# Graph attention on one core: sorted edges in groups of 128 instead of 256, and twice as many additions to the blocks' sums

## The chip, the cores and the metric

One core of a Trainium2 chip (trn2) runs the whole program. The metric is its time on the device in microseconds; the profile calls the engines PE (TensorE), DVE (VectorE), ACT (ScalarE), POOL (GpSimd) and SP (SyncE).

## What is computed

Two graph layers on 6250 nodes of 64 values with 200,000 directed edges; `dst` comes sorted, `src` doesn't. The change lies in the first, an attention over 400,000 entries (each edge both ways):

```python
idx = concatenate([edge_index, edge_index[:, ::-1]])      # 400,000 entries
src, dst = idx[:, 0], idx[:, 1]
gl, gr = (h @ Wl.T)[src], (h @ Wr.T)[dst]                 # 4 heads of 16
score = (att * leaky_relu(gl + gr, 0.2)).sum(-1)          # per head
ex = exp(score - segment_max(score, src)[src])
out = segment_sum(gr * ex / segment_sum(ex, src)[src], src)
x = x + gelu(concat([out, h]) @ W1.T + b1) @ W2.T + b2
```

The second layer sums `h[src] + edge_attr` by `dst` and ends with a normalisation over the nodes. The change leaves it alone.

## The kernel before

*Preparation and sort* (`prepare`, `Sort`, `decode`; up to about 1066 us). The entries are sorted on the chip by source node. Nodes stand in 49 blocks of 128. The entries of a block are filled up with padding to a whole number of groups of GROUP = 256, so that each group belongs to one block. `prepare` counts the entries of each block, adds them up to `ends`, and works out the block of each of the 1612 groups: a transpose of `ends` to a column, a comparison of 49 partitions with 1612 group numbers, four matmuls with ones, a limit, and a conversion to integers in `m.blk_i`, one partition (L383 to L389 on TensorE, L480 to L488 on VectorE).

*Attention* (`attention`, about 1066 to 5258 us). A step is 1024 sorted entries in 8 tiles of 128, and there are 403 steps in 13 chunks: twelve of 32 and one of 19. A score step q does this:

- GpSimd gathers the rows of `gr` by 8 indirect DMAs into one of 8 slots, tile by tile (L855).
- SyncE reads the block number of each of the 4 groups into a register and loads that block's `gl` table, 32 KB (L864, L866), up to 8 steps ahead.
- VectorE makes `hot_t`, one column of 128 for each entry (`hot_of`, L1010), four steps ahead (LAG); TensorE multiplies it with the table (`left`, L876) into bank q % 4.
- VectorE adds the gathered rows (L1062), ScalarE multiplies by the slope, VectorE takes the maximum (L1068), weighs with `att` (L1079) and sums over each head (the reduction of L139).

After the score steps of a chunk come a `scan` (the maximum of each node and the exponentials, L1085 to L1149) and then, during the score steps of the next chunk, the sum steps r of this one: weights to PSUM (`weight_of`, L1026), terms (`term_of`, L1035 and L1037), `hot_sum` (L1042), a matmul for each tile (`scatter`, L886) that sums a group over its two tiles, and one addition of 128x68 for each group into `m.acc` at the block of the group (`accumulate`, L1021). A score step takes one sum step along; a chunk with more sum steps than score steps has further ones in between (`sum_step`). The additions of step r are done at step r + 4. At a chunk's end those of its last four steps are done at once.

Each addition is made of these lines; the block number is read (L1017) right before it, and it waits for the addition before it:

```python
for i in groups:
    g = r * STEP_GROUPS + i
    blk = dve.value_load(m.blk_i[0:1, g:g + 1], min_val=0, max_val=BLOCKS - 1)
    sums = m.acc[:, bass.ds(blk, 1), :].rearrange("p b f -> p (b f)")
    at_least(dve, s_acc, g)
    dve.wait_ge(s_sum, r + 1)
    dve.tensor_tensor(sums, sums, sums_of(r % SUM_SLOTS, i), ALU.add).then_inc(s_acc, 1)
```

In `score_step` one addition follows each of four operations: the terms, L1068, `hot_of`, `hot_sum`. The sums of a step fill one of three banks (4 to 6); `scatter` of step r waits until the additions of step r - 3 are done. The scan uses banks 5 and 6 when all additions are through. The order on every engine is the order of the program text; semaphores stand for all dependences.

Of the kernel before, what the change touches and what calls it, by code (L numbers as in the profile page):

```python
# [24 lines left out]
P = 128  # L25
# [19 lines left out]
GROUP_TILES = 2  # L45
# [8 lines left out]
STEP_GROUPS = 4  # L54
STEP_TILES = STEP_GROUPS * GROUP_TILES
STEP = STEP_TILES * P
SIZES = [32] * 12 + [19]
# [84 lines left out]
def build(nc, t, out, stop=None):  # L142
    with ExitStack() as whole:
# [41 lines left out]
        m.blk_i = sb("blk_i", [1, GROUPS], I32)  # L185
        m.blk_f = sb("blk_f", [1, GROUPS], F32)
# [42 lines left out]
def prepare(m, ctx, sort):  # L229
# [16 lines left out]
    end_col = sb("end_col", [BLOCKS, 1], F32, ctx)  # L246
# [7 lines left out]
    iota_group = sb("iota_group", [BLOCKS, GROUPS], F32, ctx)  # L254
    past = sb("past", [BLOCKS, GROUPS], F32, ctx)
# [19 lines left out]
    s_end, s_end_ps = sem("s_end"), sem("s_end_ps")  # L275
    s_past, s_past_ps = sem("s_past"), sem("s_past_ps")
# [6 lines left out]
    with nc.Block() as block:  # L283
        @block.sync
        def _(sp):
            sp.wait_ge(s_init, 1)
            load_blocks(sp, m.x, t["x"], s_x)
            sp.wait_ge(s_init, 2)
            for dram, tile in ((t["src"], m.src), (t["dst"], m.dst)):
                sp.dma_start(tile[:, 0:FULL_COLS].rearrange("p (g t) -> p g t", t=EDGE_TILES),  # L290
                             dram[0:FULL_EDGES].rearrange("(g p t) -> p g t", p=P, t=EDGE_TILES)).then_inc(s_edges, 16)
                sp.dma_start(tile[0:TAIL_PARTS, FULL_COLS:EDGE_COLS],
                             dram[FULL_EDGES:E].rearrange("(p t) -> p t", t=EDGE_TILES)).then_inc(s_edges, 16)
            sp.wait_ge(s_init, 3)
# [3 lines left out]
            sp.wait_ge(s_grt, 32)  # L298

# [35 lines left out]
        def _(pool):  # L335
# [6 lines left out]
            pool.iota(iota_group[:, :], [[1, GROUPS]], base=0, channel_multiplier=0,  # L342
# [15 lines left out]
        def _(pe):  # L358
# [23 lines left out]
            pe.wait_ge(s_end, 1)  # L382
            pe.transpose(bank[6][0:BLOCKS, 0:P], ends[:, :], m.ident[:, :]).then_inc(s_end_ps, 1)  # L383
            pe.wait_ge(s_past, 1)
            part = GROUPS // 4
            for i in range(4):
                last = pe.matmul(bank[4 + i][:, 0:part], m.ones[0:BLOCKS, :], past[:, i * part:(i + 1) * part],
                                 start=True, stop=True)
            last.then_inc(s_past_ps, 1)  # L389
# [3 lines left out]
        def _(dve):  # L393
# [71 lines left out]
            dve.tensor_tensor_scan(ends[:, :], m.ones[:, 0:BLOCKS], counts[:, :], 0.0, ALU.mult,  # L465
                                   ALU.add).then_inc(s_end, 1)
# [17 lines left out]
            part = GROUPS // 4  # L484
            for i in range(4):
# [260 lines left out]
def attention(m, ctx):  # L746
# [13 lines left out]
    hot_t = [sb(f"hot_t{k}", [P, STEP], F32, ctx) for k in range(LAG)]  # L760
# [72 lines left out]
    def sums_of(slot, i):  # L833

        return bank[4 + slot][:, i * HEADS * ACCW:(i + 1) * HEADS * ACCW]
# [9 lines left out]
    with nc.Block() as block:  # L845
# [24 lines left out]
        def _(pe):  # L870
            def left(q):

                pe.wait_ge(s_hot, q + 1)
                pe.wait_ge(s_gl[q % U], loads(q, U) * STEP_GROUPS)
                for g in range(STEP_TILES):
                    last = pe.matmul(bank[q % LAG][:, g * D:(g + 1) * D], hot_t[q % LAG][:, g * P:(g + 1) * P],  # L876
                                     gl_s[q % U][:, g // GROUP_TILES, :], start=True, stop=True)
                last.then_inc(s_left, 1)
# [39 lines left out]
            for q in range(LAG):  # L918
                left(q)
            for c in range(CHUNKS + 1):  # L920
                for q, sums in turn_steps(c):
                    if q is not None and q + LAG < STEPS:
                        left(q + LAG)
# [11 lines left out]
        def _(act):  # L935
# [25 lines left out]
            for q in range(LAG + 2):  # L961
                load_place(q)
# [23 lines left out]
            for c in range(CHUNKS + 1):  # L986
                for q, sums in turn_steps(c):
                    if q is not None:
                        load_place(q + LAG + 2)
                        keep(q)  # L990
                        act.wait_ge(s_z, q + 1)
                        nc.scalar.mul(left_of(q % LAG), z[:, :, :], SLOPE).then_inc(s_low, 1)  # L992
# [7 lines left out]
        def _(dve):  # L1000
# [4 lines left out]
            def hot_of(q):  # L1005
# [4 lines left out]
                dve.tensor_tensor(hot_t[q % LAG][:, :], place_b[q % V][:, :], node_ps.to_broadcast([P, STEP]),  # L1010
                                  ALU.is_equal).then_inc(s_hot, 1)
# [32 lines left out]
            def sum_step(r, base):  # L1044

                weight_of(r, base)
                term_of(r)
                if r - LAG >= base:
                    accumulate(r - LAG, (0, 1))
                hot_sum_of(r)  # L1050
                if r - LAG >= base:
                    accumulate(r - LAG, (2, 3))

            def score_step(q, c, r, base):
# [3 lines left out]
                if r is not None:  # L1058
                    weight_of(r, base)
                dve.wait_ge(s_left, q + 1)  # L1060
# [99 lines left out]
            for q in range(LAG):  # L1160
                hot_of(q)

            for c in range(CHUNKS + 1):
# [469 lines left out]
```

## Time and profile before

| | us |
|---|---|
| median of 3 runs | 7368.41 (7367.21 to 7369.56) |
| profiled execution | 7364.49 |
| its span, first to last instruction | 7362.5 |
| VectorE busy | 4363.1 (59%) |
| GpSimd busy | 4625.4 (63%) |
| TensorE busy, matmuls | 4204.2 (57%) |
| attention, first table load to last addition | 1065.9 to 5257.8 |

Shares of busy time are means over stages of different kinds. Register and semaphore instructions of an engine's queue are not counted as busy; where they hold an engine up, it shows as idle time before the next instruction. A line of a group of instructions gives busy time and the mean of one; behind the bar stands the idle time of the engine in front of them and what ended it. TensorE's granted clock in the attention is 0.50, its lower level of 1.2 GHz.

### The profile page before, as it was taken

The page shows a single profiled execution, that of the slowest core. Times are in us where ns is not written, and L with a number is a line of the kernel's source. Part 1 is how long each engine was busy: PE and PEld are TensorE (multiplying, and loading weights), DVE is VectorE, ACT ScalarE, POOL GpSimd, SP SyncE. Part 2 cuts the span into 40 slices and gives each one's busy share as a digit, 9 for nine tenths or more (in the row PEclk, how much of TensorE's full clock was granted, in tenths as well). Part 3 has the DMA queues.
Part 4 walks back from the last instruction along what each step waited for, and adds up shares of the span by engine and source line. Part 5 has one row for each costly group of instructions (what it writes and reads, how often), then busy time and mean ns, then how long its engine had stood idle before and what let it go on. Part 6 is the DMA issues. An engine that isn't in the chain of part 4 may idle for free. (4 is left out here: it accounts for less than half of the span.)

```text
span 7362.5 us, 75948 instructions
## 1 busy us (share of the span) xinstructions
PE 4204.2 (57%) x18919; PEld 4018.0 (55%) x18919; DVE 4363.1 (59%) x7419; ACT 702.3 (10%) x1007; POOL 4625.4 (63%) x4809
## 2 busy tenths in 40 slices
PE   2011114567676777776677776768634445565666
PEld 1011114566676766666676766668533444555665
DVE  9999973667676676767667676768612222222332
ACT  6201100000000000000000000000100000000001
POOL 0000047777777777777777777775077777777774
PEclk9975555555555555555555555555655555555555
DMA  2000024444444444444444444443122222222221
GB/s 36 0 0 0 0 58 102 111 119 120 107 129 109 125 118 118 117 115 123 105 131 117 119 118 117 121 103 113 52 52 53 53 53 55 52 53 52 55 53 30
DMA packets 631935, 600.55 MB, mean 82 GB/s; under 512 B 382434, under 2 KB 385634, under 8 KB 631222
## 3 DMA queue, kind: packets, MB, share of 16 engines
q10 hardware_dynamic: 177888, 320.64, 13.7%
q0 software_dynamic: 153344, 157.33, 11.8%
q1 hardware_dynamic: 300246, 117.47, 6.4%
q8 instruction: 167, 2.74, 0.2%
q14 instruction: 290, 2.38, 0.1%
HBM read 480.76 MB, written 114.19 MB: 81 GB/s over the span
## 5 line engine op out<-in xcount | busy, mean ns | idle before, releaser
L855 POOL DMA_INDIRECT rows<-gr_table,row_of x3192 | 3075.4, 963 | 976.4 <-issue 970.8
L886 PE MATMUL bank<-terms,hot_sum 128*128 128x68 f32 x6448 | 1467.9, 423 | 774.2 <-DVE acc L1021 770.3
L886 PEld LDWEIGHTS bank<-terms,hot_sum 128*128 128x128 f32 x6448 | 1409.1, 331 | 822.6 <-DVE hot_sum L1042 817.1
L1371 POOL DMA_INDIRECT edge_rows<-h_table,src_sb x1568 | 1480.8, 944 | 531.4 <-issue 477.5
L876 PE MATMUL bank<-gl_step,hot_t 128*128 128x64 f32 x6448 | 1458.6, 421 | 280.5 <-DVE hot_t L1010 191.7
L876 PEld LDWEIGHTS bank<-gl_step,hot_t 128*128 128x128 f32 x6448 | 1421.5, 333 | 291.4 <-DVE hot_t L1010 278.3
L1392 PE MATMUL bank<-message,edge_hot 128*128 128x64 f32 x3136 | 714.6, 423 | 877.4 <-DVE message L1454 877.4
L1392 PEld LDWEIGHTS bank<-message,edge_hot 128*128 128x128 f32 x3136 | 683.5, 330 | 908.5 <-issue 908.5
L1062 DVE TENSOR_TENSOR fore<-bank,rows 128x512 f32<-128x512 f32 x403 | 277.7, 689 | 1037.0 <-DMA rows<-gr_table,row_of 1034.9
L1454 DVE TENSOR_TENSOR message<-bank,edge_rows 128x512 f32<-128x512 f32 x196 | 135.5, 692 | 1071.3 <-DMA edge_rows<-h_table,src_sb 1068.6
L696 POOL DMA_INDIRECT rows<-gr_table,row_of x32 | 50.1, 1567 | 958.5 <-DVE row_of L727 949.0
L992 ACT ACTIVATE bank<-fore 128x512 f32<-128x512 f32 x403 | 242.5, 602 | 3376.6 <-DVE fore L1062 3376.6
L1042 DVE TENSOR_TENSOR hot_sum<-bank,place 128x1024 f32<-128x1024 f32 x403 | 490.6, 1217 | 0.2 <-issue 0.2
L1010 DVE TENSOR_TENSOR hot_t<-place_b,bank 128x1024 f32<-128x1024 bf16 x403 | 489.1, 1214 | 1.5 <-DMA place_b<-place_rows 1.0
L1021 DVE TENSOR_TENSOR acc<-acc,bank 128x68 f32 x1612 | 354.2, 220 | 183.4 <-DVE acc L1021 133.8
L639 PE MATMUL bank<-ident,keys 128*128 128x128 f32 x448 | 95.9, 403 | 589.8 <-DVEq L624 500.4
L639 PEld LDWEIGHTS bank<-ident,keys 128*128 128x128 f32 x448 | 86.8, 216 | 599.8 <-DVEq L624 506.2
L1392 PE MATMUL bank<-message,edge_hot_more 128*128 128x64 f32 x1536 | 340.3, 423 | 50.4 <-DVE edge_hot_more L1423 50.4
L1392 PEld LDWEIGHTS bank<-message,edge_hot_more 128*128 128x128 f32 x1536 | 331.2, 332 | 59.4 <-DVE edge_hot_more L1423 59.4
L139 DVE TENSOR_REDUCE scores<-top 128x32 f32<-128x512 f32 x403 | 276.5, 686 | 59.5 <-DVE top L1079 1.0
L1417 ACT COPY bank<-edge 128x512 f32<-128x512 f32 x196 | 115.4, 589 | 1839.9 <-DVE message L1454 1823.2
L1068 DVE TENSOR_TENSOR fore<-fore,bank 128x512 f32<-128x512 f32 x403 | 274.5, 681 | 21.3 <-ACT bank L992 21.3
(267 smaller groups left out, 3211.9 us busy)
## 6 DMA issues: line engine op xcount, KB each, us to landing
place_b<-place_rows ACTq DMA_DIRECT2D x403, 256.0 KB
gr_rows<-rows ACTq DMA_DIRECT2D x403, 256.0 KB, 2.1
rows_again<-gr_rows ACTq DMA_DIRECT2D x403, 256.0 KB
rows<-gr_table,row_of POOLq DMA_INDIRECT x3224
gl_step<-gl_table SPq DMA_DIRECT2D x1612, 32.0 KB
edge<-in_edge_attr SPq DMA_DIRECT2D x97, 512.0 KB, 3.5
edge_rows<-h_table,src_sb POOLq DMA_INDIRECT x1568, 2.5
pen_s<-pen_rows ACTq DMA_DIRECT2D x52, 64.0 KB
```

Of the source, the lines that this page charges most:

```text
L139: return dve.tensor_reduce(out, in_, AX.X, op)
L855: pool.indirect_dma_start(rows[k][:, g, :], None, m.gr_table[:, :], bass.IndirectOffsetOnAxis(m.row_of[:, tile:tile + 1], 0)).then_inc(s_g ...
L876: last = pe.matmul(bank[q % LAG][:, g * D:(g + 1) * D], hot_t[q % LAG][:, g * P:(g + 1) * P], gl_s[q % U][:, g // GROUP_TILES, :], start=T ...
L886: last = pe.matmul(sums_of(r % SUM_SLOTS, g // GROUP_TILES), hot2[r % LAG][:, g, :], by_tile[:, g, :], start=g % GROUP_TILES == 0, stop=g ...
L992: nc.scalar.mul(left_of(q % LAG), z[:, :, :], SLOPE).then_inc(s_low, 1)
L1010: dve.tensor_tensor(hot_t[q % LAG][:, :], place_b[q % V][:, :], node_ps.to_broadcast([P, STEP]), ALU.is_equal).then_inc(s_hot, 1)
L1021: dve.tensor_tensor(sums, sums, sums_of(r % SUM_SLOTS, i), ALU.add).then_inc(s_acc, 1)
L1042: dve.tensor_tensor(hot2[r % LAG][:, :, :], places, at, ALU.is_equal).then_inc(s_summed, 1)
L1062: dve.tensor_tensor(z[:, :, :], left_of(q % LAG), rows[q % U][:, :, :], ALU.add).then_inc(s_z, 1)
L1068: dve.tensor_tensor(leaky[:, :, :], z[:, :, :], left_of(q % LAG), ALU.max).then_inc(s_leaky, 1)
L1371: pool.indirect_dma_start(rows[h % U][:, e, :], None, m.h2_table[:, :], bass.IndirectOffsetOnAxis(m.src[:, tile:tile + 1], 0)).then_inc(s_ ...
L1392: done = pe.matmul(out[:, 0:D], one_hot[:, e, :], messages_s[g % V][:, way, e, :], start=first and e == 0, stop=last and e == HALF - 1)
```

## The change

A group has 128 entries instead of 256 and a step 8 groups of one tile instead of 4 of two. A step stays 1024 entries. With smaller groups there is less padding: 397 steps instead of 403, the last chunk has 13 instead of 19, and 3176 groups stand for 1612.

- Each tile's matmul in `scatter` now stands alone, and each of the 8 groups has an addition of its own; SyncE loads 8 tables a step.
- The 8 sums of a step don't fit one bank; they take two, so there are two slots (banks 3 to 6) for three, and `scatter` of r waits for the additions of r - 2. The `left` products have three slots (LEFT) for four, with `hot_t` made three steps ahead.
- The additions of a score step stand in pairs at the four old places. The block numbers of a pair are read before the operation that the pair follows: for the first pair behind `weight_of`, for the others right behind the pair before. In `sum_step` there are two runs of four.
- The block of a group is found by comparing 25 group numbers on each of 128 partitions with the 49 ends, a reduction and a limit; a small DMA of SyncE brings the result to one partition. The transpose, the matmuls and the four limits on one partition go.

The core of the diff:

```diff
-GROUP_TILES = 2
+GROUP_TILES = 1
-STEP_GROUPS = 4
+STEP_GROUPS = 8
-SIZES = [32] * 12 + [19]
+SIZES = [32] * 12 + [13]
 LAG = 4
+LEFT = 3
-SUM_SLOTS = 3
+SUM_SLOTS = 2
+PART_GROUPS = -(-GROUPS // P)
...
-            dve.wait_ge(s_end_ps, 1)
-            c.link(dve.tensor_copy(end_col[:, :], bank[6][0:BLOCKS, 0:1]))
-            dve.tensor_scalar(past[:, :], iota_group[:, :], end_col[:, 0:1], None, ALU.is_ge).then_inc(s_past, 1)
-            dve.wait_ge(s_past_ps, 1)
-            part = GROUPS // 4
-            for i in range(4):
-                c.link(dve.tensor_scalar(m.blk_f[:, i * part:(i + 1) * part], bank[4 + i][0:1, 0:part],
-                                         float(BLOCKS - 1), None, ALU.min))
-            c.link(dve.tensor_copy(m.blk_i[:, :], m.blk_f[:, :]))
+            c.link(dve.tensor_tensor(past[:, :, :], iota_group[:, :].unsqueeze(2).to_broadcast([P, PART_GROUPS, BLOCKS]),
+                                     ends[:, :].unsqueeze(1).to_broadcast([P, PART_GROUPS, BLOCKS]), ALU.is_ge))
+            c.link(nc_reduce(dve, block_f[:, :], past[:, :, :]))
+            dve.tensor_scalar(block_of[:, :], block_f[:, :], float(BLOCKS - 1), None, ALU.min).then_inc(s_block, 1)
...
+            sp.wait_ge(s_block, 1)
+            sp.dma_start(m.blk_i[0:1, :].rearrange("o (p g) -> o p g", p=P), block_of[:, :]).then_inc(s_block_row, 16)
...
     def sums_of(slot, i):
-        return bank[4 + slot][:, i * HEADS * ACCW:(i + 1) * HEADS * ACCW]
+        half = STEP_GROUPS // 2
+        return bank[3 + 2 * slot + i // half][:, i % half * HEADS * ACCW:(i % half + 1) * HEADS * ACCW]
...
-            def accumulate(r, groups):
-                for i in groups:
-                    g = r * STEP_GROUPS + i
-                    blk = dve.value_load(m.blk_i[0:1, g:g + 1], min_val=0, max_val=BLOCKS - 1)
+            def blocks_of(r, groups):
+                return [dve.value_load(m.blk_i[0:1, r * STEP_GROUPS + i:r * STEP_GROUPS + i + 1], min_val=0, max_val=BLOCKS - 1)
+                        for i in groups]
+            def accumulate(r, groups, blocks):
+                dve.wait_ge(s_sum, r + 1)
+                for i, blk in zip(groups, blocks):
                     sums = m.acc[:, bass.ds(blk, 1), :].rearrange("p b f -> p (b f)")
-                    at_least(dve, s_acc, g)
-                    dve.wait_ge(s_sum, r + 1)
+                    at_least(dve, s_acc, r * STEP_GROUPS + i)
                     dve.tensor_tensor(sums, sums, sums_of(r % SUM_SLOTS, i), ALU.add).then_inc(s_acc, 1)
...
             def score_step(q, c, r, base):
                 if r is not None:
                     weight_of(r, base)
+                if add:
+                    blocks = blocks_of(r - LAG, (0, 1))
                 dve.wait_ge(s_left, q + 1)
                 dve.wait_ge(s_gath[q % U], loads(q, U) * STEP_TILES)
-                dve.tensor_tensor(z[:, :, :], left_of(q % LAG), rows[q % U][:, :, :], ALU.add).then_inc(s_z, 1)
+                dve.tensor_tensor(z[:, :, :], left_of(q % LEFT), rows[q % U][:, :, :], ALU.add).then_inc(s_z, 1)
                 if r is not None:
                     term_of(r)
                 if add:
-                    accumulate(r - LAG, (0,))
+                    accumulate(r - LAG, (0, 1), blocks)
+                    blocks = blocks_of(r - LAG, (2, 3))
                 dve.wait_ge(s_low, q + 1)
-                dve.tensor_tensor(leaky[:, :, :], z[:, :, :], left_of(q % LAG), ALU.max).then_inc(s_leaky, 1)
+                dve.tensor_tensor(leaky[:, :, :], z[:, :, :], left_of(q % LEFT), ALU.max).then_inc(s_leaky, 1)
                 if add:
-                    accumulate(r - LAG, (1,))
+                    accumulate(r - LAG, (2, 3), blocks)
+                    blocks = blocks_of(r - LAG, (4, 5))
-                hot_of(q + LAG)
+                hot_of(q + LEFT)
                 if add:
-                    accumulate(r - LAG, (2,))
+                    accumulate(r - LAG, (4, 5), blocks)
+                    blocks = blocks_of(r - LAG, (6, 7))
                 if r is not None:
                     hot_sum_of(r)
                 if add:
-                    accumulate(r - LAG, (3,))
+                    accumulate(r - LAG, (6, 7), blocks)
...
                     for r in range(START[c] - LAG, START[c]):
-                        accumulate(r, range(STEP_GROUPS))
+                        accumulate(r, range(STEP_GROUPS), blocks_of(r, range(STEP_GROUPS)))
```

## Rows read from the trace of the kernel before

**Rows 1.** Three stretches: us; busy PE, PEld, DVE, ACT, POOL; clock, DMA share, GB/s.

```profile
1377.70:4965.20 3587.50, 2532.07 (x11528) 2470.38 (x11528) 2431.51 (x4941) 264.74 (x407) 2725.71 (x2828) 0.50 0.45 118
4965.20:5175.20 210.00, 169.54 (x776) 165.72 (x776) 169.80 (x381) 15.33 (x24) 112.28 (x119) 0.50 0.36 104
5175.20:5257.80 82.60, 68.72 (x304) 66.05 (x304) 55.62 (x153) 0.91 (x1) 0.00 (x0) 0.50 0.17 49
```

**Rows 2.** Groups by line, 1100 to 5050: busy, mean ns | idle before, releasers.

```profile
L855 POOL DMA_INDIRECT rows<-gr_table,row_of x3114 | 3001.8, 964 | 949.1 <-issue 947.3 <-DVE fore L1062 1.8
```

**Rows 3.** Waits, 1100 to 5050: us in total, times, longest us.

```profile
DVE fore L1062 <- DMA rows<-gr_table,row_of: 1034.9, 292, 5.5
```

**Rows 4.** Line L1062, 4640 to 4664, then 1377 to 4966: durations; first, last start.

```profile
L1062 DVE TENSOR_TENSOR fore<-bank,rows x5: 680/681/687, 4640.9 to 4663.8; 128x512 f32<-128x512 f32 x5
...
L1062 DVE TENSOR_TENSOR fore<-bank,rows x353: 679/692/712, 1377.7 to 4965.2; 128x512 f32<-128x512 f32 x177
```

**Rows 5.** Timeline of VectorE after a scan: start us, us, instruction.

```profile
4676.58 0.68 DVE L1062 TENSOR_TENSOR fore<-bank,rows 128x512 f32<-128x512 f32 x1
4677.88 0.22 DVE L1021 TENSOR_TENSOR acc<-acc,bank 128x68 f32 x1
4678.01 0.68 DVE L1068 TENSOR_TENSOR fore<-fore,bank 128x512 f32<-128x512 f32 x1
...
4678.89 1.22 DVE L1010 TENSOR_TENSOR hot_t<-place_b,bank 128x1024 f32<-128x1024 bf16 x1
...
4681.43 0.68 DVE L1079 TENSOR_TENSOR top<-fore,bank 128x512 f32<-128x512 f32 x1
4682.25 0.69 DVE L139 TENSOR_REDUCE scores<-top 128x32 f32<-128x512 f32 x1
4682.95 0.68 DVE L1062 TENSOR_TENSOR fore<-bank,rows 128x512 f32<-128x512 f32 x1
```

**Rows 6.** Timeline of VectorE, first and last addition at a chunk's end.

```profile
4926.32 0.23 DVE L1021 TENSOR_TENSOR acc<-acc,bank 128x68 f32 x1 [0.15 <-issue]
...
4938.77 0.22 DVE L1021 TENSOR_TENSOR acc<-acc,bank 128x68 f32 x1 [0.60 <-DVE acc L1021]
```

**Rows 7.** Line L1088, the scan's first, 4640 to 5200.

```profile
L1088 DVE CAST edge_cols<-pen_s x2: 153/154/154, 4939.0 to 5150.7; 128x1 f32<-128x1 bf16 x2
```

**Rows 8.** Timeline of VectorE in the last sums.

```profile
5224.83 0.69 DVE L1035 TENSOR_TENSOR terms<-rows_again,bank 128x512 f32<-128x512 f32 x1
...
5227.81 0.22 DVE L1021 TENSOR_TENSOR acc<-acc,bank 128x68 f32 x1
5228.22 0.22 DVE L1021 TENSOR_TENSOR acc<-acc,bank 128x68 f32 x1 [0.19 <-DVE acc L1021]
...
5228.68 0.69 DVE L1035 TENSOR_TENSOR terms<-rows_again,bank 128x512 f32<-128x512 f32 x1
```

**Rows 9.** VectorE's queue, lines L1017, L1020 and L1021, whole span.

```profile
L1017 DVEq TENSOR_LOAD <-blk_i x1612: 296/303/992, 1402.8 to 5256.8; - x180
L1017 DVEq FUSED_REGOPS  x1612: 183/183/210, 1403.4 to 5257.2; - x180
L1017 DVEq SEQ_ASSERT  x1612: 23/23/41, 1403.7 to 5257.4; - x180
...
L1020 DVEq EVENT_SEMAPHORE  x1611: 21/21/21, 1404.6 to 5257.5; - x179
...
L1021 DVEq FUSED_REGOPS  x1612: 64/64/71, 1403.8 to 5257.5; - x180
```

**Rows 10.** TensorE's queue, line L1357, 5328 to 5331, two readings in a row.

```profile
L1357 PEldq TENSOR_LOAD <-step_of x2: 306/402/497, 5328.9 to 5329.7; - x2
```

**Rows 11.** Timeline of SyncE's queue, 1100 to 1115.

```profile
1100.34 14.76 SPq L866 DMA_DIRECT2D gl_step<-gl_table  x14
```

**Rows 12.** Timeline of the preparation, VectorE.

```profile
244.10 0.15 DVE L481 COPY end_col<-bank 49x1 f32<-49x1 f32 x1
...
254.60 0.27 DVE L552 TENSOR_TENSOR keys<-keys 128x64 f32<-128x64 f32 x1
```

More of the change, by code:

```diff
@@ L253, in prepare @@
     bias = sb("bias", [P, BLOCKS], F32, ctx)
-    iota_group = sb("iota_group", [BLOCKS, GROUPS], F32, ctx)
-    past = sb("past", [BLOCKS, GROUPS], F32, ctx)
+    iota_group = sb("iota_group", [P, PART_GROUPS], F32, ctx)
+    past = sb("past", [P, PART_GROUPS, BLOCKS], BF16, ctx)
+    block_f = sb("block_f", [P, PART_GROUPS], F32, ctx)
+    block_of = sb("block_of", [P, PART_GROUPS], I32, ctx)
     ordinal = sb("ordinal", [P, GROUP_TILES], F32, ctx)
@@ L381, in _ @@
             pe.matmul(bank[5][:, 0:BLOCKS], m.ones[:, :], below[:, :], start=True, stop=True).then_inc(s_cnt_ps, 1)
-            pe.wait_ge(s_end, 1)
-            pe.transpose(bank[6][0:BLOCKS, 0:P], ends[:, :], m.ident[:, :]).then_inc(s_end_ps, 1)
-            pe.wait_ge(s_past, 1)
-            part = GROUPS // 4
-            for i in range(4):
-                last = pe.matmul(bank[4 + i][:, 0:part], m.ones[0:BLOCKS, :], past[:, i * part:(i + 1) * part],
-                                 start=True, stop=True)
-            last.then_inc(s_past_ps, 1)
             sort.tensor(pe)
@@ L464, in _ @@
             c.link(dve.tensor_scalar(counts[:, :], counts[:, :], 1.0 / GROUP, None, ALU.mult))
-            dve.tensor_tensor_scan(ends[:, :], m.ones[:, 0:BLOCKS], counts[:, :], 0.0, ALU.mult,
-                                   ALU.add).then_inc(s_end, 1)
+            c.link(dve.tensor_tensor_scan(ends[:, :], m.ones[:, 0:BLOCKS], counts[:, :], 0.0, ALU.mult, ALU.add))
             dve.wait_ge(s_const, 6)
@@ L759, in attention @@
     place_b = [sb(f"place_b{k}", [P, STEP], BF16, ctx) for k in range(V)]
-    hot_t = [sb(f"hot_t{k}", [P, STEP], F32, ctx) for k in range(LAG)]
+    hot_t = [sb(f"hot_t{k}", [P, STEP], F32, ctx) for k in range(LEFT)]
     gl_s = [sb(f"gl_step{k}", [P, STEP_GROUPS, D], F32, ctx) for k in range(U)]
@@ L875, in left @@
                 for g in range(STEP_TILES):
-                    last = pe.matmul(bank[q % LAG][:, g * D:(g + 1) * D], hot_t[q % LAG][:, g * P:(g + 1) * P],
+                    last = pe.matmul(bank[q % LEFT][:, g * D:(g + 1) * D], hot_t[q % LEFT][:, g * P:(g + 1) * P],
                                      gl_s[q % U][:, g // GROUP_TILES, :], start=True, stop=True)
@@ L916, in scan @@
                 last.then_inc(s_back_ps, 1)
-            for q in range(LAG):
+            for q in range(LEFT):
                 left(q)
@@ L921, in _ @@
                 for q, sums in turn_steps(c):
-                    if q is not None and q + LAG < STEPS:
-                        left(q + LAG)
+                    if q is not None and q + LEFT < STEPS:
+                        left(q + LEFT)
                     for r in sums:
@@ L959, in keep @@
                               rows[q % U][:, :, :].rearrange("p g f -> p (g f)")).then_inc(s_store[q % U], 16)
-            for q in range(LAG + 2):
+            for q in range(LEFT + 2):
                 load_place(q)
@@ L1009, in hot_of @@
                 dve.wait_ge(s_place[q % V], loads(q, V))
[L1010 removed]
+                dve.tensor_tensor(hot_t[q % LEFT][:, :], place_b[q % V][:, :], node_ps.to_broadcast([P, STEP]),
                                   ALU.is_equal).then_inc(s_hot, 1)
[L1013 to L1017 removed]
+            def blocks_of(r, groups):
[4 more added lines that the diff above has]
+                for i, blk in zip(groups, blocks):
                     sums = m.acc[:, bass.ds(blk, 1), :].rearrange("p b f -> p (b f)")
[L1019 to L1020 removed]
+                    at_least(dve, s_acc, r * STEP_GROUPS + i)
                     dve.tensor_tensor(sums, sums, sums_of(r % SUM_SLOTS, i), ALU.add).then_inc(s_acc, 1)
@@ L1044, in sum_step @@
             def sum_step(r, base):
+                add = r - LAG >= base
                 weight_of(r, base)
+                if add:
+                    blocks = blocks_of(r - LAG, range(4))
                 term_of(r)
-                if r - LAG >= base:
-                    accumulate(r - LAG, (0, 1))
+                if add:
+                    accumulate(r - LAG, range(4), blocks)
+                    blocks = blocks_of(r - LAG, range(4, 8))
                 hot_sum_of(r)
-                if r - LAG >= base:
-                    accumulate(r - LAG, (2, 3))
+                if add:
+                    accumulate(r - LAG, range(4, 8), blocks)
             def score_step(q, c, r, base):
@@ L1059, in score_step @@
                     weight_of(r, base)
+                if add:
+                    blocks = blocks_of(r - LAG, (0, 1))
                 dve.wait_ge(s_left, q + 1)
                 dve.wait_ge(s_gath[q % U], loads(q, U) * STEP_TILES)
-                dve.tensor_tensor(z[:, :, :], left_of(q % LAG), rows[q % U][:, :, :], ALU.add).then_inc(s_z, 1)
+                dve.tensor_tensor(z[:, :, :], left_of(q % LEFT), rows[q % U][:, :, :], ALU.add).then_inc(s_z, 1)
                 if r is not None:
@@ L1159, in _ @@
             chain.link(dve.memset(inits[:, :, :], -BIG))
-            for q in range(LAG):
+            for q in range(LEFT):
                 hot_of(q)
```

16 lines of the change are left out of this document (6 added, 10 removed).

## The prediction

> **What bounds the kernel now.** I read the stages first [rows 1]. The first row is chunks 1 to 11 of the attention, 352 steps in 3587.5 us; the next is chunk 12 with its scan, the last the sums that are left. Then comes GpSimd's line for this stage [rows 2]: 3114 gathers, busy 3001.8 us, idle 949.1, nearly all of it issue (947.3) and only 1.8 us for a buffer. A gather therefore costs 1.27 us, a step of eight 10.15 us, and GpSimd is never held: it sets the pace of chunks 0 to 11. The list of waits says the same from VectorE's side [rows 3]: 1034.9 us of waiting for rows, about 86 us for each of the 12 chunks or so that the window holds. That is all the room the change has on VectorE before VectorE sets the pace.
>
> Where a chunk has its room is seen from the starts of the first operation of a score step (L1062). Just after a scan the gathers are ahead and VectorE runs unhindered: four steps without additions to acc take 22.9 us, 5.7 each [rows 4]; a step with four additions takes 6.37 (4676.58 to 4682.95) [rows 5]. Later it waits, and the chunk comes out at 3587.5 / 11 = 326.1 us [rows 1, 4].
>
> In chunk 12 and after it things differ: 185.5 us from its first score step (4965.2) [rows 4] to its scan (5150.7) [rows 7], where GpSimd is busy 112 of 210 us and VectorE 170 [rows 1]. VectorE's own work sets the time there, and afterwards no gather is left at all.
>
> **The change, part by part.** *Fewer steps.* 403 become 397: 48 gathers less, 48 x 1.27 = 61 us of GpSimd. All of them come off chunk 12 (19 steps become 13), which GpSimd does not bound. Its 32 sum steps stay. What can be gained there is VectorE's time alone.
>
> *Additions, 1612 to 3176.* Today one addition stands between two large operations and delays the next by 0.13 us (4677.88 to 4678.01), since its block number is read while the large operation ahead of it runs [rows 5]. In the change they come in pairs, and the second waits on s_acc until the first is done. The trace has that once nearly bare: 0.41 us from start to start (5227.81 to 5228.22) [rows 8]. From below, a dependent pair without an address (L1079 to L139) leaves 0.14 us after the end [rows 5], so 0.22 + 0.14 = 0.36. I take 0.39.
>
> *Where the block numbers are read.* This decides the forecast. A reading is three instructions on VectorE's queue: 0.303 + 0.183 + 0.023 = 0.509 us [rows 9]. The old order is: large operation, reading, addition. The new one is: additions, two readings, large operation. A large operation is handed over only when both readings in front of it are through, and they can't start early, because in front of them stands the address of the second addition, which waits for the first. So 0.22 us of addition is all the engine has to cover two readings. What an uncovered reading costs is seen at a chunk's end, where 16 additions stand with nothing between: 12.45 / 15 = 0.83 us each, 0.60 of it idle [rows 6]. Of the 0.83, 0.021 + 0.064 are the wait and the address [rows 9], so a reading is between 0.51 and 0.74; I take the middle, 0.62. Two in a row don't overlap on TensorE's queue, where the one such place has them 0.8 us apart [rows 10].
>
> From the second addition to the next large operation is thus 0.83 - 0.09 + 0.62 = 1.36 us, where it was 0.13. Each of the first three pairs adds 0.39 + 1.36 - 0.13 = 1.62; the fourth, with no readings behind it, 0.39. The first pair's readings stand behind the copy of the weights, beside the last reduction: from that reduction's start to the next L1062 took 0.70 us (4682.25 to 4682.95) [rows 5] and will take 0.1 + 1.24 + 0.1 = 1.44, so 0.74 more. A score step goes from 6.37 to 6.37 + 4.86 + 0.39 + 0.74 = 12.36 us. That is above the gathers' 10.15: VectorE becomes the bound and GpSimd waits.
>
> The Trainium skill, Perfetto Trace Analysis (Per-engine timelines), says that a VectorE instruction waits for semaphores in a queue of its own while the sequencer goes on, but that an instruction of the sequencer alone holds it until its semaphores are there. By the first half alone the readings would run ahead and the step would stay under the gathers' time (rival 1); the second half goes with the forecast, as L1021 has a register operation of its own ahead of each addition [rows 9].
>
> *A chunk.* Four steps without additions 22.9; 27 periods of 12.36, 333.7; from the last L1062 to the end of its reduction 12.36 - 1.44 + 0.69 = 11.6. At the chunk's end four steps are added at once: each 8 x 0.62 + 0.2 + 7 x 0.39 = 7.9, together 31.6 (13 today, 16 x 0.83). From scan start (4939.0) to the next chunk (4965.2) 26.2 as now [rows 4, 7]. Sum 426 for 326.1, times 11: +1099 us.
>
> *Chunk 12.* Two steps without additions 11.4, eleven with 136.0. A sum step takes 3.85 today (5224.83 to 5228.68) [rows 8]; less its additions (0.83, 0.41 and twice 0.13) 2.35 of other work. With eight readings, 4.96, and two runs of four additions, 6 x 0.39 = 2.34, it takes 9.65; 17 of them 164, two without additions 4.7; the end 31.6, less 1.4 for one head too many: 346 for 185.5, +161. *After it,* 13 sum steps: 4 x 2.35 + 9 x 9.65 + 31.6 = 128 for 82.6 [rows 1], +45.
>
> *Left slots three, sum banks in two slots.* The sums of step r now wait for the additions of r - 2 instead of r - 3, and behind them in TensorE's queue stands the next left product. TensorE is busy 2532 / 352 = 7.2 us a step [rows 1]: sums and left product are through some 7.3 us after those additions, and VectorE asks for them after the rest of that step (2.4) and a whole further one (12.36). Cost nothing; with a step of 7.9 (rival 1) still covered, by 3 us.
>
> *Table loads, eight a step.* SyncE, when nothing holds it, issues one every (14.76 - 0.33) / 13 = 1.11 us [rows 11], 8.9 a step: under 10.15 and 12.36, so hidden, except in chunk 0, where VectorE has no sums to do. There 32 x 8.9 = 284 us put the last scores some 10 us later than now: +10, between 0 and 20. The 51 MB more fit beside a DMA share of 0.45 [rows 1].
>
> *Blocks of the groups.* The stretch from 244.10 to 254.60 [rows 12] becomes a comparison and a reduction of 1225 elements (1.4 us each by L1010's 1.22 for 1024 [rows 5]) and a clamp of 0.2: 10.5 less 3.0, -7.5. The row's DMA has the whole sort as cover.
>
> Sum: 1099 + 161 + 45 + 10 - 7.5 = +1307 us, on the profiled execution's 7364.5 us; the median shown lies 3.9 above it: 8675 us.
>
> **The rivals.** *1. Readings hidden.* If the queue runs ahead, a step is 6.37 + 4 x 0.39 = 7.9, under 10.15, and eleven chunks stay at 326. Chunk 12: 11.4 + 11 x 7.9 + 4.7 + 17 x 4.7 + 31.6 = 215, +29; after it 9.4 + 9 x 4.7 + 31.6 = 83, nothing; with -7.5: 7390. For it: readings do run under large operations today [rows 5]. Against: there they stand behind one in the order.
>
> *2. Readings in a row cheaper.* [...] If each costs the 0.30 of the load alone [rows 9], a step is 12.36 - 8 x 0.32 = 9.8 and a chunk 22.9 + 264.6 + 56 = 343.5, +191; chunk 12 is 256 readings x 0.32 = 82 shorter, +79; after it 33 shorter, +12: 7368 + 275 = 7643. Against: the checks stand after every load [rows 9].
>
> *3. Faster.* If each added addition costs 0.13 and readings nothing anywhere, a score step is 6.9 and a sum step 2.35 + 8 x 0.13 = 3.4: chunk 12 is 11.4 + 75.9 + 4.7 + 57.8 + 13 = 163, -22; after it 9.4 + 30.6 + 13 = 53, -30; with -7.5: 7309. It decides while the additions of the 37 steps there cost under 1.6 us a step more than that; the idle 0.60 at the chunk's end [rows 6] speaks against it.
>
> **How the numbers follow.** Forecast 0.86, rival 1 0.05, rival 2 0.05, rival 3 0.02, within 0.2% (about what a measurement tells from no change) 0.02. Within the forecast every one of 3176 readings is bare: 0.51 for 0.62 takes 350 us off, 0.36 for 0.39 some 50; 0.74 would add 380, which I cut to 225, since the gaps between register operations are short. Range 8300 to 8900. Faster 0.03, same 0.03, slower 0.94.
>
> **What the profile would show.** Right: L1062's starts 12 us apart in mid-chunk and no wait for rows after a chunk's first steps; GpSimd idle with L1062 as releaser, some 100 us a chunk; three gaps of over 1 us a step, before leaky, hot_t and hot_sum; 0.39 us inside a pair. Wrong: L1062 still waiting for gathers at a period of 10 us (rivals 1 and 3), or gaps of 0.6 us (rival 2). TensorE's sums at the front of the waits would mean that the two slots have become the bound. The forecast is furthest off if the second address doesn't hold the queue.

## The result, and the profile after

The changed kernel takes 8602.5 us (median of 4 runs, 8601.4 to 8603.9) where the kernel before took 7369.0 beside it: a ratio of 1.167 [1.165, 1.169]. It is 1233 us slower; the forecast was 8675 in a range of 8300 to 8900. Some executions, of the kernel before too, are about 40 us longer than the rest; where a profile caught one (the kernels with one reading and without the range check below), TensorE's granted clock stayed at 0.50 in the 50 us behind the attention's last addition, for 0.92 to 0.94 in the others, and the second layer's first gather came 111 us behind that addition instead of 72.

The page of the changed kernel, its span and the groups that answer to the rows of before (columns: busy us, mean ns | idle before, and what ended most of it). L855 of before is L846 here, L1068 L1069, L1010 L1001, L1042 L1036 and L1021 L1015; L1062 has kept its number:

```profile
span 8599.6 us, 92355 instructions
...
L846 POOL DMA_INDIRECT rows<-gr_table,row_of x3144 | 2972.9, 946 | 2068.6 <-issue 1347.2
L877 PE MATMUL bank<-terms,hot_sum 128*128 128x68 f32 x6352 | 1449.2, 423 | 1909.5 <-DVE acc L1015 1906.0
...
L1036 DVE TENSOR_TENSOR hot_sum<-bank,place 128x1024 f32<-128x1024 f32 x397 | 485.7, 1223 | 403.3 <-issue 403.3
L1001 DVE TENSOR_TENSOR hot_t<-place_b,bank 128x1024 f32<-128x1024 bf16 x397 | 483.9, 1219 | 389.6 <-issue 388.1
...
L1069 DVE TENSOR_TENSOR fore<-fore,bank 128x512 f32<-128x512 f32 x397 | 272.9, 687 | 374.2 <-issue 352.9
L1062 DVE TENSOR_TENSOR fore<-bank,rows 128x512 f32<-128x512 f32 x397 | 274.1, 690 | 350.9 <-issue 202.7
```

Before, GpSimd was never held and VectorE waited 1034.9 us for rows [rows 2, 3]. Now GpSimd's gathers (L846) are idle 2068.6 us, and four large VectorE operations have 350 to 400 us of idle time each ahead of them. The releaser named is mostly "issue": no engine and no transfer was late, VectorE's own queue was. TensorE's sums wait 1906.0 us for additions, but these waits bind nothing, because VectorE never waits for a sum. What its additions waited for in chunks 1 to 11, and the longest wait of GpSimd there that isn't issue (us, times, longest):

```profile
POOL rows L846 <- DMA gr_rows<-rows: 626.4, 98, 60.3
...
DVE acc L1015 <- issue: 214.2, 44, 5.3
...
DVE acc L1015 <- DVE acc L1015: 6.5, 13, 0.5
```

The three stages that answer to [rows 1], from the same views (us; busy PE, PEld, DVE, ACT, POOL; clock, DMA share, GB/s):

```profile
1407.43:6015.33 4607.90, 2545.36 (x11528) 2474.62 (x11528) 2799.78 (x6349) 264.58 (x407) 2668.77 (x2828) 0.50 0.37 102
6015.33:6374.40 359.07, 156.46 (x696) 149.89 (x696) 181.37 (x479) 11.65 (x18) 37.72 (x40) 0.50 0.14 44
6374.40:6497.20 122.80, 47.28 (x208) 45.27 (x208) 49.91 (x157) 0.96 (x1) 0.00 (x0) 0.50 0.07 20
```

In chunks 1 to 11 VectorE's busy time grew by 368 us (1408 more instructions, all small additions), and the stage by 1020. The granted clock is the same 0.50 (1.2 GHz). So about two thirds of the loss is idle time of VectorE, not work.

One score step in mid-chunk, VectorE's timeline (start us, us, instruction, idle before; "x2" is a pair of additions):

```profile
4000.44 0.59 DVE L1015 TENSOR_TENSOR acc<-acc,bank 128x68 f32 x2
4002.09 1.22 DVE L1036 TENSOR_TENSOR hot_sum<-bank,place 128x1024 f32<-128x1024 f32 x1 [1.05 <-issue]
4003.23 0.59 DVE L1015 TENSOR_TENSOR acc<-acc,bank 128x68 f32 x2
...
4004.56 0.69 DVE L141 TENSOR_REDUCE scores<-top 128x32 f32<-128x512 f32 x1
...
4005.94 0.69 DVE L1062 TENSOR_TENSOR fore<-bank,rows 128x512 f32<-128x512 f32 x1 [0.59 <-issue]
...
4008.87 0.69 DVE L1069 TENSOR_TENSOR fore<-fore,bank 128x512 f32<-128x512 f32 x1 [1.04 <-issue]
...
4011.33 1.22 DVE L1001 TENSOR_TENSOR hot_t<-place_b,bank 128x1024 f32<-128x1024 bf16 x1 [1.27 <-issue]
```

VectorE's queue between the pair at 4000.44 and hot_sum at 4002.09, lines L1006 (readings) and L1015 (the addition's address), durations and first and last start:

```profile
L1006 DVEq TENSOR_LOAD <-blk_i x2: 301/302/304, 4000.8 to 4001.5; - x2
L1006 DVEq FUSED_REGOPS  x2: 190/190/190, 4001.2 to 4001.8; - x2
L1006 DVEq SEQ_ASSERT  x2: 23/23/23, 4001.4 to 4002.0; - x2
...
L1015 DVEq FUSED_REGOPS  x2: 64/64/64, 4000.7 to 4002.2; - x2
```

Read the two together. The address of the second addition stands at 4000.7, when the first addition is done; the first load starts at 4000.8, the last range check ends at 4002.0, and hot_sum starts at 4002.09. Two readings stand there, one after the other, with no large operation beside them. The gaps are the three that the prediction named, ahead of hot_sum, leaky (L1069) and hot_t, and a smaller one ahead of L1062.

### The profile page after: what moved, and what is told of

Read it like the earlier page. It is cut to its first block and busy times, and to the rows that moved or that the text cites. A ratio compares the mean times of both kernels' runs of the same rounds, so it can differ in the third digit from the quotient of the medians.

```text
span 8599.6 us, 92355 instructions
## 1 busy us (share of the span) xinstructions
PE 4171.6 (49%) x18718; PEld 3978.6 (46%) x18718; DVE 4734.8 (55%) x8925; ACT 698.6 (8%) x1001; POOL 4518.1 (53%) x4761
## 5 line engine op out<-in xcount | busy, mean ns | idle before, releaser
L846 POOL DMA_INDIRECT rows<-gr_table,row_of x3144 | 2972.9, 946 | 2068.6 <-issue 1347.2
L877 PE MATMUL bank<-terms,hot_sum 128*128 128x68 f32 x6352 | 1449.2, 423 | 1909.5 <-DVE acc L1015 1906.0
L877 PEld LDWEIGHTS bank<-terms,hot_sum 128*128 128x128 f32 x6352 | 1385.4, 330 | 1969.0 <-DVE hot_sum L1036 1768.0
L867 PE MATMUL bank<-gl_step,hot_t 128*128 128x64 f32 x6352 | 1436.8, 421 | 322.9 <-DMA gl_step<-gl_table 268.1
L867 PEld LDWEIGHTS bank<-gl_step,hot_t 128*128 128x128 f32 x6352 | 1400.5, 333 | 333.3 <-issue 273.7
L1015 DVE TENSOR_TENSOR acc<-acc,bank 128x68 f32 x3176 | 702.5, 221 | 527.1 <-issue 257.4
L1036 DVE TENSOR_TENSOR hot_sum<-bank,place 128x1024 f32<-128x1024 f32 x397 | 485.7, 1223 | 403.3 <-issue 403.3
L1001 DVE TENSOR_TENSOR hot_t<-place_b,bank 128x1024 f32<-128x1024 bf16 x397 | 483.9, 1219 | 389.6 <-issue 388.1
L686 POOL DMA_INDIRECT rows<-gr_table,row_of x32 | 50.1, 1565 | 954.4 <-DVE row_of L717 944.9
L1069 DVE TENSOR_TENSOR fore<-fore,bank 128x512 f32<-128x512 f32 x397 | 272.9, 687 | 374.2 <-issue 352.9
L1062 DVE TENSOR_TENSOR fore<-bank,rows 128x512 f32<-128x512 f32 x397 | 274.1, 690 | 350.9 <-issue 202.7
L1029 DVE TENSOR_TENSOR terms<-rows_again,bank 128x512 f32<-128x512 f32 x397 | 268.9, 677 | 56.1 <-issue 54.6
```

The source lines that it names most:

```text
L846: pool.indirect_dma_start(rows[k][:, g, :], None, m.gr_table[:, :], bass.IndirectOffsetOnAxis(m.row_of[:, tile:tile + 1], 0)).then_inc(s_g ...
L867: last = pe.matmul(bank[q % LEFT][:, g * D:(g + 1) * D], hot_t[q % LEFT][:, g * P:(g + 1) * P], gl_s[q % U][:, g // GROUP_TILES, :], start ...
L877: last = pe.matmul(sums_of(r % SUM_SLOTS, g // GROUP_TILES), hot2[r % LAG][:, g, :], by_tile[:, g, :], start=g % GROUP_TILES == 0, stop=g ...
L1001: dve.tensor_tensor(hot_t[q % LEFT][:, :], place_b[q % V][:, :], node_ps.to_broadcast([P, STEP]), ALU.is_equal).then_inc(s_hot, 1)
L1029: dve.tensor_tensor(term[:, :, 0:DH], rows2[r % V][:, :, :].rearrange("p g (h f) -> p (g h) f", f=DH), weight_ps[r % 2].unsqueeze(2).to_br ...
L1036: dve.tensor_tensor(hot2[r % LAG][:, :, :], places, at, ALU.is_equal).then_inc(s_summed, 1)
```

## The experiments

**All readings gone.** Every group's sums are added to one block, whose number is read once. This leaves out the blocks of the groups, and with them the address ahead of each addition.

```
-  return [dve.value_load(m.blk_i[0:1, r * STEP_GROUPS + i:...], ...) for i in groups]
+  return [one_block for _ in groups]
```

> The changed kernel, but one block number is read once, ahead of the attention, and all 3176 additions go to that block (left out: the block of each group, and with it the address worked out before each addition; the sums land in the wrong block). Theory, bare readings set the time: a score step falls from 12.1 us to about 6.37 + 4 x 0.37 = 7.8, below the gathers' 10.15, so chunks 1 to 11 go back to 326 us each and the whole to about 7360 us (7340 to 7380). Rival, the doubled additions with their waits, the two sum slots or the eight table loads set it: the step stays near 12 us and the time above 8400.

Measured: 7328.0 us (10 runs), 0.993 [0.991, 0.996] of the kernel before. All 3176 additions, the smaller slots and the table loads are still there, and the kernel is 1274 us faster than the changed one. Two rows of its waits, 1100 to 5050 (us, times, longest; L1061 is L1062 of before):

```profile
POOL rows L846 <- issue: 943.8, 3094, 0.3
...
DVE fore L1061 <- DMA rows<-gr_table,row_of: 568.9, 223, 3.6
```

GpSimd sets the pace again and VectorE waits for rows. Chunks 2 and on last about 326 us, as before. The gain over before comes at the end: chunk 12 takes 173 us to its scan and the sums after it 58, for 185.5 and 82.6 [rows 1, 4, 7]. The time came out 12 us under the expectation's range. A step just after a scan takes 7.2 us where it reckoned with 7.8 and a dependent pair at 0.37 from start to start; without an address instruction the pair's starts are some 0.25 apart, 0.47 from first start to last end:

```profile
4506.34 0.47 DVE L1014 TENSOR_TENSOR acc<-acc,bank 128x68 f32 x2
4506.73 0.68 DVE L1068 TENSOR_TENSOR fore<-fore,bank 128x512 f32<-128x512 f32 x1
4507.33 0.48 DVE L1014 TENSOR_TENSOR acc<-acc,bank 128x68 f32 x2
4507.72 1.21 DVE L1001 TENSOR_TENSOR hot_t<-place_b,bank 128x1024 f32<-128x1024 bf16 x1
```

**The same readings in the old order.** Each pair's two readings stand behind the large operation and ahead of their additions; nothing else is changed.

```
-      accumulate(r - LAG, (2, 3), blocks)
-      blocks = blocks_of(r - LAG, (4, 5))
+      accumulate(r - LAG, (2, 3), blocks_of(r - LAG, (2, 3)))
```

> The changed kernel with all of its readings, each pair read behind the large operation that its additions follow instead of ahead of it. Theory: two readings take 1.24 us and now run under 1.2 us (terms, hot_t, hot_sum) or 0.6 us (leaky); a score step is about 9.5 us, a chunk 345 (326.1 before), a sum step about 8.2; time about 7750 us (7650 to 7850). Rival, the number of readings counts and not their place: unchanged, 8600 us. Rival, any cover hides them whole: a step under 8 us, time under 7420.

Measured: 7817.8 us, 1.059 [1.054, 1.065]. The same 3176 checked readings cost 785 us less for their place alone. The idle time that is left now stands ahead of the additions (here for 1400 to 5250) and no longer ahead of the large operations:

```profile
L1015 DVE TENSOR_TENSOR acc<-acc,bank x2808: 224/226/227, 1434.9 to 5247.0; 128x68 f32 x188
its engine sat idle before it (us, times) until:
  issue: 659.7, 922
```

A large operation of 1.22 us nearly covers its pair's 1.24 us of readings (0.15 us of idle time ahead of the pair behind hot_sum, 0.31 behind hot_t, both means); leaky, one of 0.68 us, does not (0.79). A step takes about 9.7 us, a chunk 351 to 355.

**The readings without their range check.** A reading is then the load alone.

```
-  dve.value_load(..., min_val=0, max_val=BLOCKS - 1)
+  nc.s_assert_within(dve.value_load(...), 0, BLOCKS - 1, skip_runtime_bounds_check_because="...")
```

> The changed kernel in its own order, with the range check of a reading (two of its three instructions, some 0.29 us of 0.62) left out on VectorE; the numbers are the same. Theory, every reading is bare: 3176 x 0.29 = 920 us less until the gathers hold again: step 9.8 us, chunk 345, time about 7690 us (7600 to 7800). Rival, readings cost nothing and the second addition's wait or TensorE's two slots set the step: 8500 or more.

Measured: 7837.7 us, 1.062 [1.056, 1.068], above the expected range. In the profiled execution 39 us of that lie behind the attention (111 us to the second layer's first gather, for 72 in the changed kernel), where the edit changes nothing; without them it would be at the range's upper end. That readings set the step is borne out (765 us less, about 800 between the profiled executions without those 39), but not 0.29 us for each. The large operations from 1400 to 5300:

```profile
L1001 DVE TENSOR_TENSOR hot_t<-place_b,bank x352: 1214/1221/1223, 1412.8 to 5265.3; 128x1024 f32<-128x1024 bf16 x176
its engine sat idle before it (us, times) until:
  issue: 309.1, 308
...
L1037 DVE TENSOR_TENSOR hot_sum<-bank,place x352: 1218/1225/1226, 1413.9 to 5267.5; 128x1024 f32<-128x1024 f32 x176
its engine sat idle before it (us, times) until:
  issue: 154.0, 308
```

Ahead of hot_sum 0.50 us (154.0 / 308), as two loads of 0.31 less some cover make it; ahead of hot_t 1.00. One of the two loads there often takes three times as long as the others. This is taken up below.

**One load for a pair.** A pair's two numbers (four or eight in the sums) come with one unchecked load into as many registers.

```
-  return [nc.s_assert_within(dve.value_load(...), ...) for i in groups]
+  return nc.values_load_multi_w_load_instructions(m.blk_i[0:1, lo:lo + len(groups)], ...)[1]
```

> The changed kernel in its own order, unchecked, with the block numbers of a pair (of four in a sum step, of eight at a chunk's end) read by one load into several registers. Theory: if such a load takes as long as a single one (0.30 us), 0.4 us stand bare ahead of a large operation instead of 1.27, a step is about 8.7 us, the gathers hold again and the time is about 7390 us (7360 to 7420). If it takes 0.30 us for each number, it is the unchecked kernel again, 7650 to 7700 us.

Measured: 7568.6 us, 1.027 [1.022, 1.032]: between the two answers. Such a load of two numbers took 0.53 us, one of eight 0.60, against 0.30 for one; ahead of hot_t the load of two took 1.19 (median). The loads and hot_t from 1400 to 5100:

```profile
L1007 DVEq TENSOR_LOAD <-blk_i x1275: 520/530/1451, 1434.7 to 5096.4; - x183
...
L1001 DVE TENSOR_TENSOR hot_t<-place_b,bank x352: 1214/1221/1223, 1414.0 to 5085.0; 128x1024 f32<-128x1024 bf16 x176
...
  issue: 266.4, 308
```

Ahead of hot_t VectorE is idle 0.86 us (266.4 / 308). A step takes about 9.7 us, a chunk 336 to 341.

**One load of eight, covered.** All eight numbers of a step come with one unchecked load, behind the operations of the terms; the additions stay in pairs.

```
+      blocks = blocks_of(r - LAG, range(8))
       accumulate(r - LAG, (0, 1), blocks)
-      blocks = blocks_of(r - LAG, (2, 3))
...
-      accumulate(r - LAG, (2, 3), blocks)
-      blocks = blocks_of(r - LAG, (4, 5))
+      accumulate(r - LAG, (2, 3), blocks[2:])
```

> The changed kernel with one unchecked load of all eight block numbers of a step behind the terms, so no reading stands bare; the pairs and runs of additions stay. Theory: a score step about 7.85 us, gathers hold chunks 1 to 11 at 326 us, a sum step about 5.3 us; chunk 12 to its scan about 206 us (185.5 before, 334.6 in the change), after it 71 (82.5 before); time about 7365 us (7345 to 7385). Rival, something else of the change costs in every chunk: 7450 us or more.

Measured: 7358.0 us (12 runs), 0.999 [0.997, 1.001]. Everything of the change is in this kernel except the place, the number and the range check of its readings, and it takes the time of the kernel before. Its waits from 1100 to 5050 (L1059 is L1062 of before) read as before, with less room:

```profile
POOL rows L846 <- issue: 944.7, 3099, 0.3
...
DVE fore L1059 <- DMA rows<-gr_table,row_of: 412.7, 196, 3.2
```

**The additions spread.** As the last kernel, but the load stands behind the copy of the weights, and the additions stand singly between large operations where there is room, so that few additions wait for a neighbour.

> The same with the load behind the copy of the weights and the additions of a score step one at a time between large operations (one pair is left), those of a sum step in two pairs and a run of four, so that few wait bare for the one before. Theory: a score step about 7.1 us, a sum step 4.6, chunk 12 to its scan about 186 us, after it 64; time about 7340 us (7320 to 7360), faster than both. Rival, the waits between additions cost nothing beside large operations: the same as the kernel with one load.

Measured: 7361.2 us, 1.000 [0.998, 1.002]: no gain over the kernel with one load, where 7340 was expected. A score step did get shorter (7.2 us for 7.7 after a scan), but there gathers set the time. In chunk 12 and behind it the sum steps set it, and one of them takes 4.85 us (5051.46 to 5056.31), no less than in the kernel with one load (4.81, 5051.41 to 5056.22), where 4.6 was expected:

```profile
5051.46 0.69 DVE L1032 TENSOR_TENSOR terms<-rows_again,bank 128x512 f32<-128x512 f32 x1
5052.30 0.59 DVE L1016 TENSOR_TENSOR acc<-acc,bank 128x68 f32 x2 [0.15 <-issue]
5052.81 0.20 DVE L1037 COPY terms<-bank 128x32 f32<-128x32 f32 x1
5053.11 0.59 DVE L1016 TENSOR_TENSOR acc<-acc,bank 128x68 f32 x2
5053.62 1.22 DVE L1052 TENSOR_TENSOR hot_sum<-bank,place 128x1024 f32<-128x1024 f32 x1
```

The load now shows (0.15 of idle time), and pairs and, behind hot_sum, a run of four are still there: a sum step has too few large operations for eight single additions.

**The kernel before with three left slots and two sum banks.** The same edit as in the change, alone.

> The kernel before (groups of 256, 403 steps) with the change's slots alone: three left products and two slots of sums, so that the sums of a step wait for the additions two steps back. Theory: TensorE is done 7.3 us after those additions, earlier than VectorE asks; no change, 7367 us (7355 to 7380), steps just after a scan at most 7.3 us instead of 6.4. Rival, the two slots hold the steps: a step over 10.15 us, 7600 us or more.

Measured: 7378.8 us, 1.002 [1.000, 1.005]: at most a small loss. A step is as before, but from a chunk's last L1062 to its scan it takes 25.4 us where it took about 19.5, and the gathers' room takes up most of that, not all: in the profiled execution 9 us are lost when chunk 12 begins (4974.2 for 4965.2), and 12 at the last addition.

**The kernel before with each table loaded twice.** Eight loads a step on SyncE's queue, as in the change.

> The kernel before with each table loaded twice, eight loads a step as in the change. Theory: SyncE's queue sets chunk 0 alone (about 335 us from its first score step to that of chunk 1, where it is 300 now), and as the gathers run on they take it back in chunk 1; 7367 us (7355 to 7385). Rival, the loads or their traffic slow the gathers in every chunk: 7450 us or more.

Measured: 7364.7 us, 0.999 [0.997, 1.001]. Chunk 0 takes 344.6 us for 300.5, and chunks 1 and 2 take 303 and 313 where they took 340 and 324: GpSimd gathers on meanwhile, and the 44 us are given back. This holds only while gathers set the pace; in the changed kernel, where VectorE does, nothing is given back (chunk 1 takes 420 us, chunk 2 419).

**The transfers issued later.** For the slow load ahead of hot_t two answers stood: its place in the order, or the three 256 KB transfers that ScalarE issues just ahead of it. In the kernel with one load per pair ScalarE now waits for the step's hot_t before it issues them.

```
  nc.scalar.mul(left_of(q % LEFT), z[:, :, :], SLOPE).then_inc(s_low, 1)
+ act.wait_ge(s_hot, min(q + LEFT + 1, STEPS))
```

> The kernel with one load per pair, and one wait more on ScalarE's queue: after its product of a step it waits for that step's hot_t before it issues the three 256 KB transfers of the next steps. In the kernel with one load per pair the load ahead of hot_t took 1.19 us and the others 0.53, and the three transfers were issued just ahead of it. Theory: the transfers slow the load. Then the load ahead of hot_t falls to about 0.53, the idle time ahead of hot_t from a mean of 0.87 us to about 0.38, and the slow load moves to a later reading, that of the next step's first pair, where some of it lies beside the reduction: about 7480 us (7420 to 7550) against 7569 without the added wait. Rival: it is the place in the order, behind the second pair of additions. Then the load ahead of hot_t stays at 1.19, its idle time at 0.87, and the time at about 7569 (7550 to 7590).

Measured: 7397.0 us, 1.004 [1.001, 1.007], under the expected range; the kernel without that wait took 7568.6. Between the two profiled executions, which are alike behind the attention, the one wait is worth 152 us (7548.7 and 7397.1). From 1400 to 5100, the loads and hot_t:

```profile
L1008 DVEq TENSOR_LOAD <-blk_i x1318: 342/528/1381, 1432.4 to 5097.7; - x189
...
L1002 DVE TENSOR_TENSOR hot_t<-place_b,bank x360: 1211/1221/1223, 1411.7 to 5090.3; 128x1024 f32<-128x1024 bf16 x180
its engine sat idle before it (us, times) until:
  issue: 119.2, 314
```

Ahead of hot_t there are 0.38 us (119.2 / 314), as ahead of the other large operations. So the slow load goes with the transfers and not with the place in the order. The gain is larger than expected because the slow load did not move to the next pair, but for 11 times in all: a step takes 9.1 us, a chunk 324 to 325, and GpSimd is held no longer. What about the transfers does it stays open: a load at 4511.0 took 0.524 us while the DMA engines were 0.89 busy (4510.3 to 4512.2), so traffic alone is not enough.

## Why the prediction was right

**The bound changes and the readings do it: shown.** The order of the readings alone is worth 785 us, the readings and addresses together 1274, and with the readings covered by one load the change costs nothing. The profile shows the three gaps, 1.04 to 1.27 us, and GpSimd waiting. In all 1232 pairs of chunks 1 to 11 the register operation of the second address starts 0.04 us behind the end of the first addition, whatever stood ahead of the pair; where readings follow, the first load starts another 0.13 us later. By the Trainium skill, Perfetto Trace Analysis (Per-engine timelines), an instruction of the sequencer alone waits for its semaphores in the sequencer; the queue's rows agree (the second address at 4000.7, the next load at 4000.8). No run takes the address away and leaves the readings, since that takes the readings' use away too; the kernel with one reading shows what is left without it, a pair at 0.25 us.

**Its terms.** A reading was put at 0.62 us: the chunk's end has eight of them bare ahead of eight additions, 4.9 us of idle time, 0.61 each:

```profile
6486.64 2.80 DVE L1015 TENSOR_TENSOR acc<-acc,bank 128x68 f32 x8 [4.91 <-issue]
6494.36 2.80 DVE L1015 TENSOR_TENSOR acc<-acc,bank 128x68 f32 x8 [4.92 <-issue]
```

In the step above two loads start 0.62 apart (4000.84 and 4001.45). The bounds 0.51 and 0.74 came from rows, but that their middle is so near is luck. Eight additions with their readings take 7.72 us from one step's to the next's, where 7.9 was said. A pair's starts are 0.37 apart (2.80 is seven such and 0.22), where 0.39 was said; from the second addition's start to hot_sum 1.27 for 1.36 (to hot_t, with its slower load, 1.49); from the reduction to L1062 1.38 for 1.44. A score step is thus about 12.1 us for 12.36, and a chunk 418.9 (4607.9 / 11) for 426. That makes chunks 1 to 11 longer by 1020 us where the sum had 1099. These 79 us too many, 12 in chunk 12 and 5 behind it, less the 25 too few in chunk 0 that follow, are nearly all of the 72 us between forecast and result. Chunk 12 to its scan takes 334.6 us (6015.3 to 6349.9), 149 more for 161 said; the sums behind it 122.8, 40 more for 45.

**The term that was mis-sized: table loads in chunk 0.** The prediction had +10 us there, 20 at most; it is +35 (335.3 us to chunk 1's first L1062, for 300.5). The loads do pace that chunk, as was said, at 9.2 us a step for 8.9, and that makes 16 of the 35. What was missed is the scan behind it, the other 19. VectorE at the end of chunk 0:

```profile
1361.99 0.14 DVE L1091 CAST edge_cols<-pen_s 128x1 f32<-128x1 bf16 x1
...
1384.89 0.69 DVE L1094 COPY score_s<-bank 128x512 f32<-128x512 f32 x1 [21.63 <-PE bank L886]
...
1406.21 1.01 DVE L1150 COPY weights<-bank 128x512 f32<-128x512 f32 x1 [3.15 <-PE bank L905]
```

and TensorE's waits in it (us, times, longest):

```profile
PE bank L867 <- DMA gl_step<-gl_table: 187.0, 34, 7.0
```

The scan takes 44.2 us (1361.99 to 1406.21) where the one of before took 25.5: its products on TensorE stand behind left products, and those wait for tables. The kernel before with twice the loads shows the same by itself, a scan of 53 us.

**The blocks of the groups.** Preparation was to become 7.5 us shorter. The three instructions take 3.03 us (244.09 to 247.12), as said; at the first L1062 5.0 us are left (1072.2 for 1077.2). With the 2.2 us by which what follows the attention is shorter, the terms give 1020 + 149 + 40 + 35 - 5 - 2 = 1237 us, the difference of the two spans.

**The rivals.** Readings hidden, 7390: that is the kernel with one load (7358), not this one. Readings cheaper in a row, 7643: a checked reading costs its 0.61 us beside another too. Without the check the time is 195 us above it, 155 of them the slow load ahead of hot_t (309.1 less 154.0), most of the rest the 39 us behind the attention. Faster, 7309: the kernel with one reading comes near it (7328), so the gain is there to be had in chunk 12 and behind it, but of these kernels only the one whose additions need neither a number nor an address has it. The slots, put at nothing, do cost nothing in the changed kernel, whose additions wait for no sum; in the kernel before they cost about 0.2%, at the chunks' ends.

**The signs.** L1062's starts 12 us apart, no wait for rows in chunks 1 to 11 and the three gaps came as named. Two signs did not tell what they were said to. GpSimd is idle some 100 us more a chunk, but what ends most of its long waits is the store of a slot's rows (`gr_rows`, which ScalarE issues between its steps) and not L1062. And TensorE's sums do stand near the front of the waits, the sign for the two slots as the bound; they stand there because additions come late, and only waits of VectorE for sums would have meant the slots.

**What was not reached.** No kernel with all of the work in it was clearly faster than the one before. Fewer steps with smaller groups leave VectorE eight additions with an address each in a step; the 48 gathers saved lie where nothing waits for them.

## What to carry to other kernels

Before moving a register load in an instruction order, ask which engine instruction covers it: behind an operation as long as itself it costs little (0.15 to 0.31 us of 1.24 behind operations of 1.22), behind an instruction that itself waits it costs nearly all of its length (1.05 of 1.24). A row of "issue" ahead of large operations on an engine that is half idle is a queue that is too slow, and the remedy is fewer or better placed queue instructions (one load for eight numbers), not faster work. Where an engine has slack in most stages, look at the stage without slack for what a saving is worth, and count the loads that pace a stage also against what stands behind them there.

## What the runs showed of the hardware that was not expected

- A load of one number into a register takes 0.30 us on VectorE's queue, of two 0.53, of eight 0.60: eight numbers cost twice what one does. The Trainium skill, DMA: Bandwidth & Descriptors (Latency and other measured facts), gives such a load a floor of some 600 ns; one number is at half of it here.
- A load of two numbers behind three 256 KB transfers of ScalarE took 1.19 us in the median and up to 1.45. In the kernel with one load per pair all 231 loads of over 0.9 us in chunks 1 to 11 start 0.55 to 1.32 us behind the start of the third one's issue (the store to `gr_rows`); 75 others start there too and are not slow. With the transfers issued behind another operation the slow loads were gone from their place, and 152 us with them. Which part of a transfer's start does it is open.
- Two dependent additions follow at 0.37 us with an address worked out from a register between them, at about 0.25 with a fixed one. The address is worked out only when the first addition is done (0.04 us behind its end, in all of 1232 pairs), and what stands behind it in the queue waits with it.
